# Two unused edge tiles dropped and two VectorE products joined in a graph layer's edge loop

## The reference, cut to what matters

```python
sj = xs[idx_j]; vj = xv[idx_j]            # rows of a node table: 128 scalars, 3 x 128 vector components
h = shifted_softplus(f_ij @ Wf1 + bf1)
W = (h @ Wf2 + bf2) * rcut_ij[:, None]    # filters of the edge
m_s = s2 * W[:, :2 * F]                   # s2 holds sj and sum_i vj_i * Yv_i
m_v = (v2.reshape(e, 2 * F, 3) * W[:, 2 * F:4 * F, None]).reshape(e, 6 * F)   # sj * Yv_i and vj_i
agg = jax.ops.segment_sum(x_ij, idx_i, num_segments=n)
```

## Time and profile before

| | us |
|---|---|
| median of 3 runs (lowest, highest) | 1677.06 (1670.42, 1679.36) |
| span of the profiled execution | 1465.5 |
| first gather of the edge loop | 185.0 |
| last addition of the edge loop ends | 1061.88 |
| TensorE busy in the span | 1316.5 |
| VectorE busy | 1076.8 |
| GpSimd busy | 800.7 |

### The profile page before, as it was taken

How to read it: one execution, slowest core, us unless ns; L and a number is a source line. 1 busy time by engine, 2 the same in 40 slices (tenths; PEclk the granted TensorE clock), 3 DMA queues, 4 the chain that set the end, 5 groups by cost and what they waited for, 6 DMA issues and landing times. The chain is left out here.

```text
span 1465.5 us, 27308 instructions
## 1 busy us (share of the span) xinstructions
PE 1316.5 (90%) x7078; PEld 788.7 (54%) x7078; DVE 1076.8 (73%) x2882; ACT 840.3 (57%) x2153; POOL 800.7 (55%) x848
## 2 busy tenths in 40 slices
PE   0787779999999999999999999999881699999997
PEld 0553245555555655555555555555481455555553
DVE  6899859999999999999999999999877311111110
ACT  3679957777777777777777777777552011111111
POOL 2157577777777777777777777777300122222211
PEclk9989979999999999999999999999995699999998
DMA  6045034444444444444443444444533155555521
GB/s 242 7 190 171 1 80 112 124 128 123 122 116 125 112 140 127 126 128 124 140 114 109 112 114 109 112 113 109 87 123 132 58 161 161 160 150 153 152 43 18
DMA packets 65893, 173.20 MB, mean 118 GB/s; under 512 B 14027, under 2 KB 22619, under 8 KB 65213
## 3 DMA queue, kind: packets, MB, share of 16 engines
q0 software_dynamic: 43648, 106.09, 28.4%
q1 hardware_dynamic: 22196, 66.57, 12.8%
HBM read 149.28 MB, written 18.08 MB: 114 GB/s over the span
## 5 line engine op out<-in xcount | busy, mean ns | idle before, releaser
L1084 PE MATMUL PS<-prod,oneh 128*64 128x256 f32 x2064 | 471.7, 382 | 7.1 <-DVE region_s L912 4.9
L545 POOL DMA_INDIRECT recs<-rec_d,inv_i x344 | 325.0, 945 | 117.6 <-issue 89.6
L556 POOL DMA_INDIRECT gath<-table_d,recs x344 | 325.3, 946 | 110.2 <-issue 72.2
L1084 PEld LDWEIGHTS PS<-prod,oneh 128*64 128x64 f32 x2064 | 270.8, 137 | 202.5 <-issue 76.1
L677 ACT ACTIVATE oneh<-oneh,recs 128x64 f32<-128x64 f32 x1032 | 283.8, 337 | 136.7 <-DVE oneh L888 134.2
L1077 PE MATMUL PS<-prod,oneh 128*64 128x256 f32 x1376 | 358.6, 392 | 0.0
L1065 PE MATMUL PS<-wf_sb,h_t 128*128 128x512 f32 x688 | 334.3, 609 | 2.9 <-DVE h_t L874 2.9
L684 ACT COPY PS<-c_rep 128x512 f32<-128x512 f32 x340 | 193.4, 584 | 90.7 <-DVE prod L901 88.6
L912 DVE TENSOR_TENSOR region_s<-region_s,PS 128x512 f32 x344 | 232.6, 676 | 9.9 <-issue 6.8
L901 DVE TENSOR_TENSOR prod<-PS,gath 128x384 f32<-128x384 f32 x344 | 188.4, 548 | 0.0
L899 DVE TENSOR_TENSOR prod<-PS,gath 128x384 f32<-128x384 f32 x344 | 188.4, 548 | 0.0
(11 more groups left out here) (271 smaller groups left out, 1595.6 us busy)
## 6 DMA issues: line engine op xcount, KB each, us to landing
region_r<-wu SPq DMA_DIRECT2D x16, 512.0 KB, 4.5
region_r<-wd SPq DMA_DIRECT2D x16, 512.0 KB, 5.8
region_u<-wu SPq DMA_DIRECT2D x16, 512.0 KB, 4.5
region_u<-wd SPq DMA_DIRECT2D x16, 512.0 KB, 5.6
recs<-rec_d,inv_i POOLq DMA_INDIRECT x344
gath<-table_d,recs POOLq DMA_INDIRECT x344
region_u<-rec_in SPq DMA_DIRECT2D x1, 5168.0 KB, 17.5
rec_d<-region_u SPq DMA_DIRECT2D x1, 5168.0 KB
```

Source lines behind the costliest of these rows:

```text
L545: nc.gpsimd.indirect_dma_start(out=recs[:, q % RING, k, :], out_offset=None, in_=rec_d, in_offset=bass.IndirectOffsetOnAxis(ap=inv_i[:, t: ...
L556: nc.gpsimd.indirect_dma_start(out=gath[:, t % GRING, :], out_offset=None, in_=table_d, in_offset=bass.IndirectOffsetOnAxis(ap=recs[:, q % ...
L1084: return nc.tensor.matmul(to, oneh[:, slot, 1 + i, :], prod[:, slot, P_Q:P_B + i + 1:1 + i, :], start=i == 0, stop=i == 2, skip_group_chec ...
```

## The change

The edge loop runs 342 tiles in place of 344: `USED` counts them, the last group has `LAST` = 2 tiles, and every engine's step asks `tiles_of(left)` how many tiles a group has, where `left` is the number of groups behind it. `BODIES` falls from 28 to 27, so that the last group and those that look ahead to it are written out: five groups behind the loop, before two. `TILES` stays 344 for the sorting and the maps. The two products of vector components, of 128 x 384 each, become one of 128 x 768 whose filter operand is repeated over three components and whose row operand is repeated over the two filters.

```diff
+USED = (EDGES + BUCKETS * (P - 1)) // P
+TILES = -(-USED // QUAD) * QUAD
+LAST = USED - QUAD * (QUADS - 1)
+def tiles_of(left):
+    return QUAD if left >= 1 else LAST
-BODIES = QUADS // RING
+BODIES = (QUADS - RING) // RING
...
-                for t in range(TILES):
-                    if t + GRING < TILES:
+                for t in range(USED):
+                    if t + GRING < USED:
                         gather_record(t + GRING)
                     gather_source(t)
...
-                    nc.vector.tensor_tensor(prod[:, slot, P_D:P_D + 3, :],
-                                            w[:, W_D:W_D + 1, :].to_broadcast([P, 3, FDIM]), v, ALU.mult)
-                    nc.vector.tensor_tensor(prod[:, slot, P_B:P_B + 3, :],
-                                            w[:, W_B:W_B + 1, :].to_broadcast([P, 3, FDIM]), v, ALU.mult
-                                            ).then_inc(prod_ready, 1)
+                    nc.vector.tensor_tensor(
+                        prod[:, slot, :, :].rearrange("p (g k) f -> p g k f", g=2)[:, :, 1:4, :],
+                        w[:, W_D:W_B + 1, :].unsqueeze(2).to_broadcast([P, 2, 3, FDIM]),
+                        v.unsqueeze(1).to_broadcast([P, 2, 3, FDIM]), ALU.mult).then_inc(prod_ready, 1)
...
-                    one_hot(t + 3, r, 3, 3, body, first=first)
-                    for k in range(1, QUAD):
+                    if here == QUAD:
+                        one_hot(t + 3, r, 3, 3, body, first=first)
+                    for k in range(1, here):
                         products(t + k, r, k, k, body)
...
-                    for k in range(QUAD):
+                    for k in range(here):
                         sum_tile(QUAD * q + k, k, SUM_BANKS[(QUAD * r + k) % SRING],
```

More of the change, by code:

```diff
@@ L32 @@
 QUAD = 4
-TILES = -(-((EDGES + BUCKETS * (P - 1)) // P) // QUAD) * QUAD
+USED = (EDGES + BUCKETS * (P - 1)) // P
+TILES = -(-USED // QUAD) * QUAD
 QUADS = TILES // QUAD
+LAST = USED - QUAD * (QUADS - 1)
 TCOLS = -(-TILES // P)
@@ L552, in gather_source @@
                     if k == 0:
-                        hold(pool, recs_in[q % RING], 16 * QUAD * (q // RING + 1), pool_passed)
+                        hold(pool, recs_in[q % RING], 16 * QUAD * (q // RING) + 16 * tiles_of(QUADS - 1 - q), pool_passed)
                     if t >= GRING:
@@ L684, in seed, with step @@
                     nc.scalar.copy(ps_w[slot], c_rep[:, :]).then_inc(seeded, 1)
-                def step(q, r, left=2, first=False):
+                def step(q, r, left=RING, first=False):
                     nxt, t = (r + 1) % RING, QUAD * q + QUAD
-                    if not first:
+                    n = tiles_of(left)
+                    if not first and n == QUAD:
                         seed(t - 1, 3)
-                    for k in range(3):
+                    for k in range(min(n, 3)):
                         scaled_one_hots(t - QUAD + k, r, k, k)
@@ L694, in step @@
                         seed(t, 0)
-                    scaled_one_hots(t - 1, r, 3, 3)
+                    if n == QUAD:
+                        scaled_one_hots(t - 1, r, 3, 3)
                     if left >= 1:
@@ L699, in step @@
                         log_of_z(q + 1)
-                        seed(t + 1, 1)
-                        seed(t + 2, 2)
+                        for k in range(1, min(tiles_of(left - 1), 3)):
+                            seed(t + k, k)
                 size_of_z(0)
@@ L875, in hidden, with transpose_records, one_hot @@
                                                    in1=soft[:, 1, :], op0=ALU.max, op1=ALU.add).then_inc(h_ready, 1)
-                def transpose_records(r, body):
-                    dve.wait_ge(recs_in[r], 16 * QUAD * body + 16 * QUAD)
+                def transpose_records(r, body, n=QUAD):
+                    dve.wait_ge(recs_in[r], 16 * QUAD * body + 16 * n)
                     nc.vector.transpose(rec_t[:, r, :], recs[:, r].rearrange("p k c -> p (k c)")).then_inc(rec_t_ready, 1)
-                def one_hot(t, r, k, slot, body, first=False):
+                def one_hot(t, r, k, slot, body, first=False, n=QUAD):
                     rec = recs[:, r, k, :]
-                    dve.wait_ge(recs_in[r], 16 * QUAD * body + 16 * QUAD)
+                    dve.wait_ge(recs_in[r], 16 * QUAD * body + 16 * n)
                     if not first:
@@ L915, in flush_of, with step @@
                     flush(QUAD * q + k, SUM_BANKS[(QUAD * r + k) % SRING], first=first)
-                def step(q, r, body, left=2, first=False):
+                def step(q, r, body, left=RING, first=False):
                     nxt, nbody, t = (r + 1) % RING, body + (r + 1) // RING, QUAD * q
+                    here, then = tiles_of(left), tiles_of(left - 1)
                     products(t, r, 0, 0, body)
@@ L927, in step @@
                     if left >= 1:
-                        one_hot(t + QUAD, nxt, 0, 0, nbody)
+                        one_hot(t + QUAD, nxt, 0, 0, nbody, n=then)
                         hidden(q + 1, nxt)
+                    if here < QUAD:
+                        return
                     flush_of(q, r, 1)
                     if left >= 1:
-                        one_hot(t + QUAD + 1, nxt, 1, 1, nbody)
+                        one_hot(t + QUAD + 1, nxt, 1, 1, nbody, n=then)
                     if left >= 2:
-                        transpose_records((r + 2) % RING, body + (r + 2) // RING)
+                        transpose_records((r + 2) % RING, body + (r + 2) // RING, n=tiles_of(left - 2))
                     flush_of(q, r, 2)
-                    if left >= 1:
+                    if left >= 1 and then == QUAD:
                         one_hot(t + QUAD + 2, nxt, 2, 2, nbody)
@@ L950, in _ @@
                     step(q, q % RING, q // RING, left=QUADS - 1 - q)
-                flush_of(QUADS - 1, (QUADS - 1) % RING, 3)
+                flush_of(QUADS - 1, (QUADS - 1) % RING, LAST - 1)
             @block.tensor
@@ L1092, in sum_tile, with step @@
                     scaled(2).then_inc(s_done, 1)
-                def step(q, r, body, left=2):
-                    for k in range(QUAD):
+                def step(q, r, body, left=RING):
+                    here = tiles_of(left)
+                    for k in range(here):
                         second_layer(q, r, k, k)
```

## The result

The changed kernel took 1665.59 us in the median of 20 runs (1661.82 to 1678.39), the kernel before 1677.95 in the median of 20 (1669.16 to 1703.63): a ratio of 0.993, 95% interval 0.9903 to 0.9956, or 11.7 us less by the ratio (7.4 to 16.3). Single executions of a kernel ran some per cent longer than its others now and then; the ratios leave these out. The forecast was 1671.5 us, 5.6 less. The measured time lies inside the stated range of 1659 to 1679, 0.6 us above the low edge of the forecast's own range of 1665 to 1677, and the sign is right; the size is twice the forecast. A difference of under 0.5% had a chance of 0.77 in the prediction and one of over 0.5% a chance of 0.18; the measured 0.7% falls under the second.

The account below looks back on a forecast made before the run. GpSimd's gather issue was taken to bound the edge loop at 10.0 us a group. Two tiles less take 5.6 us off the 1465.5 span, the join nothing, 211.6 stay: 1671.5 us, range 1659 to 1679 (own range 1665 to 1677).

Parts of the forecast that it names:

- GpSimd's issues bind: Edge loop: gather issue at 1.250 us a step sets 10.0 us a group, ahead of TensorE's 9.85 and VectorE's 9.4.
- The joined product: VectorE in the edge loop: one 768-column product of 938 ns saves 0.075 us a tile, hidden by GpSimd; 0.1 us in all.
- the prediction's sign: VectorE in the loop: busy share lower by about 1.5 points, idle time ahead of L906 larger by as much.
- Two tiles less: End of the edge loop: four gathers fewer and no late-record wait, last sum at 1056.3, 5.6 us earlier; bounds 5.0 to 7.0.
- the late records' wait: Loop's end: a 1.83 us transpose wait stretches group 84 to 11.88 us on TensorE; forecast to go, leaving 9.85.
- the 211.6 around it stay: Outside the profile's span: 211.6 us of the 1677.06 us device time taken as unchanged, beside a span falling to 1459.9.
- rival 2: Edge loop: the long product holds up GpSimd's issues, slower, 133 us if one issue a tile is held (1805); chance 0.04.
- gaps above 0.3: GpSimd in the edge loop: over 0.3 us between gathers would show the long product holding up its issues.
- rival 1: Edge loop: VectorE's time is on the path after all, 19 us capped (1658) or 1645 uncapped; chance 0.14.
- The clock: Behind the loop, as the experts' work begins: half speed may return at another time, up to 1.7 us lost or won.

Follow-up runs that it names:

- the second cut: Changed kernel with the 768-column product cut into six in the first three tiles of each group: 1716.03 us, 1.0078 of the kernel before.
- its halves: Kernel before with only the product joined, 1669.47 us, ratio 0.9968; changed kernel with the product cut in two again, 342 tiles alone, 1671.0 us, ratio 0.9982.
- the four of the second chip: Changed kernel with product cut in each fourth tile, 1696.98 us; in first three, 1716.03; last 40 tiles left out, 1563.39; plain sums joined, 1683.55.

## Why the prediction was right, and where it was not

- *GpSimd's issues bind, 1.25 us a step, 10.0 us a group.* Right where the loop runs as in the profile: shown on one chip by the runs with half of the gathers left out, which end at TensorE's 9.85, and the other such chip has the same groups of 10.0. Not so on the other two chips, nor, by their times, in the 20 timed runs of each kernel: GpSimd waits there 2.4 us more in each group.
- *The joined product: 938 ns, 0.075 us saved a tile, worth nothing in the loop.* It takes 949 ns. The next instruction starts 0.86 behind it (1051.51 to 1052.37), forecast 0.855. Its gain went into waiting for rows and filters where groups take 10.0. VectorE's busy share fell by 2.5 points there; the prediction's sign said 1.5, but its own 0.3 us in 10.0 are 3. Where groups take 12.4, some 0.3 of VectorE's time counted by the second cut, which would make the join's 26 us worth up to 8; alone it gave 1.0 us by one measure and 5.4 (0.9 to 9.9) by the other.
- *Two tiles less, 5.6 us.* Right in mechanism and size under the profile's condition: the late records' wait gone, group 84 at 9.84, the last sum at 1056.64 for 1056.3, and 0.34% measured for 0.33% with the kernel that posts one update less. Where groups take 12.4, two tiles are 6.2.
- *The step that failed* is the term "the 211.6 around it stay". A span of 1465.5 beside runs of 1677 was read as 211.6 us outside the span. Only 1.7 are; some 200 lie inside it, in the edge loop (1078 us where the profile had 877), since the profile was of an execution in the other condition. That the time fell inside the range all the same is in good part luck: the bound that the sum rests on doesn't hold in the timed runs, and two tiles happen to cost nearly the same in both conditions, 6.2 us for 5.6. The terms for the timed condition, 6.2 for the tiles and something from 1 to 8 for the join, were not in it; with the scatter of the kernel before they can make up the measured 11.7, but no run shows how it divides.
- *Rivals.* The long product doesn't hold up GpSimd: the median of its gathers is 0.94 to 0.95 us after as before, in every trace with all gathers. One sign that was to speak for rival 2, gaps above 0.3, did appear, but the kernel before shows the same gaps on the same chip. VectorE on the path, rival 1, is wrong where groups take 10.0. Where they take 12.4 VectorE's time counts in part, by a mechanism that the rival didn't name; the measured 1665.6 us lies between the forecast and its 1658. The clock was right as a term behind the loop: that stretch took from 403.5 to 405.5 us over the traces, with the half-speed part at 61.4 or 64.9. Inside the loop, where the prediction had it full, it falls in the timed condition.

## What to carry to other kernels

A span and a device time that differ by more than a few us (here 1.7 in each run that has both) are a question to settle first: a profile can be of another condition than the times. An engine whose waits are all of one fixed length, here 0.3 us behind every gather, isn't idle, and its instruction count over the stretch gives its true rate. A ratio of under 1% needs the unchanged kernel run often beside it: here two sets of its runs on one chip gave 5 and 9 us for the same change. Where an issuing engine sets the pace, cutting work on the others only moves their waits; what pays is fewer issues.

## What the runs showed of the hardware

- The same kernel took 1468 to 1469 us on two chips and 1670 to 1699 on two others, all of the difference in the edge loop (877 against 1078 us; the stretch behind it is 404 us on each).
- In the longer condition the updates of TensorE's semaphores come late once in each group, only in the loop: ScalarE starts behind `first_layer`'s matmuls by 5.1 to 5.2 us in the median in the five traces of the kernel before, the changed kernel and its halves, and by 3.5 to 4.6 in the four of the second chip. The traces hold half as many semaphore updates (9,381 for the kernel before, against 19,714). Of the 10,333 missing, 9,143 are of the nine semaphores of the gathers: 1,816 in place of 10,959. The lateness ends with the gathers, too. Both point at the gathers, their updates or the recording of these, and neither shows it; whether chips, their setting, or the recording itself causes the lateness isn't told by these runs. It didn't follow from the number of TensorE's instructions; the number of updates and the gathers couldn't be tried, since the runs meant for it met chips without it.
- In that condition, where TensorE stands still for a part of each group, the granted clock falls to half for 3.4 us or a multiple in some groups (6 stretches in the loop of the changed kernel's trace); matmuls of 256 columns then take 0.63 us for 0.38.
- A gather costs GpSimd 1.25 us of issue, at 128 bytes a row as at 2048, with VectorE idle or busy.
